# Down products one place later in the period, and one half of the hidden sums moved from GpSimd to VectorE

## What is computed

```python
s0 = relu(x @ swi[0]) @ swo[0]                    # 512 -> 2048 -> 512
s1 = relu(x @ swi[1]) @ swo[1]
eo = relu(x @ wi[type_label[b]]) @ wo[type_label[b]]
gate_in = concatenate([eo[:, 0], s0[:, 0], s1[:, 0]])        # first token of each batch entry
w = softmax(relu(gate_in @ g1) @ g2)                         # 3 weights for the entry
x = x + eo * w[0] + s0 * w[1] + s1 * w[2]
x = x + x @ W[cat_ids[b]] + b[cat_ids[b]]
```

## Time and profile before

| | us |
|---|---|
| median of 3 runs | 2041.92 |
| lowest, highest | 2038.39, 2043.65 |
| profiled execution | 2036.01 |
| its span, first to last instruction | 2034.2 |

### The profile page before, as it was taken

How to read it: one execution, slowest core, us unless ns; L and a number is a source line. 1 busy time by engine, 2 the same in 40 slices (tenths; PEclk the granted TensorE clock), 3 DMA queues, 4 the chain that set the end, 5 groups by cost and what they waited for, 6 DMA issues and landing times.

```text
span 2034.2 us, 24901 instructions
## 1 busy us (share of the span) xinstructions
PE 1956.8 (96%) x8504; PEld 1603.7 (79%) x8504; DVE 1269.4 (62%) x1186; ACT 968.5 (48%) x1441; POOL 877.3 (43%) x607
## 2 busy tenths in 40 slices
PE   6999999999899999999999999998989999999998
PEld 5777777777788888888788888887768888888886
DVE  6787788687654565445744554578874655455545
ACT  5655665555553343334443444356544643334342
POOL 5757775677422232233522322366563322223223
PEclk8999999999999999999999999999999999999999
DMA  6657666766676776566686676577568866666653
GB/s 222 228 226 262 257 228 244 298 233 239 229 255 207 223 238 204 180 197 194 209 269 195 194 242 197 198 257 259 227 220 275 256 215 210 208 191 201 196 161 124
DMA packets 187024, 450.98 MB, mean 222 GB/s; under 512 B 16916, under 2 KB 57876, under 8 KB 180500
## 3 DMA queue, kind: packets, MB, share of 16 engines
q1 hardware_dynamic: 186900, 449.39, 65.3%
HBM read 308.81 MB, written 140.51 MB: 221 GB/s over the span
## 4 chain that ended last, share of the span: by engine, by line
PE 79%; DVE 7%; issue 5%; POOL 4%; DMA 3%; ACT 2%; SPq 0%; POOLq 0%; ACTq 0%; DVEq 0%
PE rps L1248 38%; PE ups L1248 37%; PE aps L1248 3%; DMA PDR<-in_L_cond_wo_dram 2%; DVE HL L963 2%; DVE WD L953 1%; POOL HT L609 1%; DVE WU L946 1%; POOL XT L556 1%; DVE ACC L980 1%; DVE XL L937 1%; DVE gacc L1027 0%; POOL XT L659 0%; DMA PDR<-in_L_cond_swo_dram 0%; DMA XT<-in_x_dram 0%
## 5 line engine op out<-in xcount | busy, mean ns | idle before, releaser
L1248 PE MATMUL rps<-HH,WD 128*128 128x512 f32 x2688 | 890.4, 393 | 39.8 <-issue 38.8
L1248 PE MATMUL ups<-XH,WU 128*128 128x512 f32 x2688 | 894.7, 393 | 33.5 <-DVE hid L993 10.0
L609 POOL TENSOR_TENSOR HT<-hid 128x512 f32<-128x512 f32 x192 | 270.0, 1406 | 957.5 <-PE rps L1248 856.3
L1248 PEld LDWEIGHTS rps<-HH,WD 128*128 128x128 f32 x2688 | 509.2, 189 | 155.3 <-issue 47.5
L1248 PEld LDWEIGHTS ups<-XH,WU 128*128 128x128 f32 x2688 | 508.7, 189 | 151.1 <-DVE hid L993 14.2
L1248 PE MATMUL ups<-XL,WU 128*128 128x512 f32 x1344 | 527.0, 392 | 0.0
L1248 PE MATMUL rps<-HL,WD 128*128 128x512 f32 x1344 | 526.7, 392 | 0.0
L963 DVE TENSOR_TENSOR HL<-HT,HH 128x1024 fp32r<-128x1024 f32 x240 | 311.9, 1320 | 50.3 <-POOL HT L609 32.8
L983 DVE SCALAR_TENSOR_TENSOR ACC<-rps,gw,ACC 128x1024 f32<-128x1024 f32 x129 | 165.4, 1282 | 281.9 <-PE rps L1248 281.9
L1248 PEld LDWEIGHTS rps<-HL,WD 128*128 128x128 f32 x1344 | 254.6, 189 | 52.3
L1248 PEld LDWEIGHTS ups<-XL,WU 128*128 128x128 f32 x1344 | 254.6, 189 | 51.9
(11 more groups left out here) (102 smaller groups left out, 1487.2 us busy)
## 6 DMA issues: line engine op xcount, KB each, us to landing
WU<-wu_kept SPq DMA_DIRECT2D x448, 256.0 KB, 3.3
WD<-wd_kept SPq DMA_DIRECT2D x224, 512.0 KB, 3.4
wd_kept<-WD SPq DMA_DIRECT2D x112, 512.0 KB, 3.1
wu_kept<-WU SPq DMA_DIRECT2D x32, 1024.0 KB, 5.8
wu_kept<-WU SPq DMA_DIRECT2D x32, 768.0 KB, 3.3
sums_kept<-ACC SPq DMA_DIRECT2D x28, 512.0 KB, 5.0
MB<-sums_kept SPq DMA_DIRECT2D x28, 512.0 KB, 5.8
PUR<-in_L_cond_swi_dram SPq DMA_DIRECT2D x16, 512.0 KB, 7.0
```

Source lines behind the costliest of these rows:

```text
L609: pool.tensor_tensor(dst, p, q, op).then_inc(s_T, 1)
L1248: ins = pe.matmul(dst, stationary[a], moving[c], start=start and j == 0, stop=stop and j == 2, skip_group_check=True)
```

## The change

The diff does four things. (1) `place_of` moves every down product, with its addition, spill, kept and loaded down weights, one place later: place i of pass m now holds product i-1 of step m, place 0 product 6 of step m-1; the very last product follows the loop. The sums of gate, mixing and first token that hang on it move with it. (2) `hidden_sum` takes the engine as an argument. The four sums of half b run on VectorE at the start of the pass, in the order 0, 1, 3, 2; those of half a stay on GpSimd, the last of them (3) now at the start of the next pass. Each half has its own semaphore. (3) The orders change: high parts 3, 2, 6, 4, 5 and low parts 3, 1, 2, 6, 4, 5; `first_down_product` stands behind `chain(a)`, `relu_11(a)` and `scale_sums`; the addition of product 6 of the step before stands behind four sums and low parts 3, 1, 2 on VectorE. On GpSimd both `up_sums` go ahead of the hidden sums, and the token sums 0 and 1 follow them, 2 goes ahead of `down_sums`. (4) `made_after` makes down weights 0 and 1 of a prepared step together at place 5 (before: at places 3 and 4), the others one product later in step with the slots; `blocks_down` and `down_sums` have waits to fit.

```diff
-HI_ORDER = [0, 1, 6, 2, 3, 4, 5]
-LO_ORDER = [0, 6, 1, 2, 3, 4, 5]
+HI_ORDER = [0, 1, 3, 2, 6, 4, 5]
+LO_ORDER = [0, 3, 1, 2, 6, 4, 5]
...
+T_COUNT = [(1, 2, 3, 4), (1, 2, 4, 3)]
...
+def place_of(m, i):
+
+    return divmod(PRODUCTS * m + i - 1, PRODUCTS)
...
+def made_after(m, i):
+
+
+    e = down_of(m, i) + WD_SLOTS
+    made = {PRODUCTS - WD_SLOTS: [], PRODUCTS - WD_SLOTS + 1: [e - 1, e]}.get(i, [e])
+    return [k for k in made if k >= 0 and prepared(k // PRODUCTS)]
...
-        s_T = sem("hidden_sums")
+        s_T = [sem("hidden_sums_0"), sem("hidden_sums_1")]
...
-                    sp.wait_ge(s_wld, PRODUCTS * PREP[N])
+                    sp.wait_ge(s_wld, PRODUCTS * PREP[N] - 1)
+                    sp.wait_ge(s_Sd, 4 * PREP[N])
...
-                    e = down_of(m, i) + WD_SLOTS
+                    e = down_of(*place_of(m, i)) + WD_SLOTS
                     if e >= 0 and e // PRODUCTS < STEPS and not prepared(e // PRODUCTS):
                         load_down(e // PRODUCTS, e % PRODUCTS)
-                    if d >= 0 and spilled(d) and i >= 1:
+                    past, which = place_of(m, i - 1)
+                    if past >= 0 and spilled(past):
                         for j in range(SUMS):
-                            if SUM_LAST[j] == i - 1:
-                                spill(d, j)
-                    if e - 1 >= 0 and prepared((e - 1) // PRODUCTS):
-                        keep_down((e - 1) // PRODUCTS, (e - 1) % PRODUCTS)
+                            if SUM_LAST[j] == which:
+                                spill(past, j)
+                    for k in made_after(past, which):
+                        keep_down(k // PRODUCTS, k % PRODUCTS)
...
+        def hidden_sum(eng, N, half, which):
...
+                eng.wait_ge(s_T[half], 4 * N + T_COUNT[half][0])
...
+            eng.tensor_tensor(dst, p, q, op).then_inc(s_T[half], 1)
...
+                if PREP[N] > 0:
+                    pool.wait_ge(s_wld, PRODUCTS * PREP[N])
...
                 if d >= 0:
-                    for which in range(4):
-                        hidden_sum(d, 1, which)
+                    hidden_sum(pool, d, 0, 3)
                 if prepared_half(2 * N + 1):
                     up_sums(2 * N + 1)
-                if N < STEPS:
-                    hidden_sum(N, 0, 0)
-                    hidden_sum(N, 0, 1)
-                if end:
-                    token_sum(pool, super_of(m) + 1, 0)
                 if prepared_half(2 * N + 2):
                     up_sums(2 * N + 2)
                 if end:
+                    token_sum(pool, super_of(m) + 1, 0)
                     token_sum(pool, super_of(m) + 1, 1)
                 if N < STEPS:
-                    hidden_sum(N, 0, 2)
+                    hidden_sum(pool, N, 0, 0)
+                    hidden_sum(pool, N, 0, 1)
+                if end:
+                    token_sum(pool, super_of(m) + 1, 2)
                 if prepared(N):
                     down_sums(N)
-                if end:
-                    token_sum(pool, super_of(m) + 1, 2)
                 if N < STEPS:
-                    hidden_sum(N, 0, 3)
+                    hidden_sum(pool, N, 0, 2)
...
                 def second(i):
 
-                    if d >= 0:
-                        begin_sum(d, i)
-                    e = down_of(m, i) + WD_SLOTS
-                    if e >= 0 and prepared(e // PRODUCTS):
+                    step, which = place_of(m, i)
+                    if step >= 0:
+                        begin_sum(step, which)
+                    for e in made_after(step, which):
                         down_high(e // PRODUCTS, e % PRODUCTS)
 
-                if d >= 0:
-                    hidden_high(d, 6)
                 if more:
                     first_product(a)
                 if d >= 0:
-                    hidden_high(d, 2)
+                    hidden_high(d, 3)
                 if more:
                     seventh_product(a)
                 if m == -1:
...
                     for i in (4, 3, 5, 6):
                         token_high(0, i)
                 if d >= 0:
-                    first_down_product(d)
-                    hidden_high(d, 3)
+                    hidden_high(d, 2)
+                if start:
+                    token_high(s + 1, 5)
                 second(0)
+                if d >= 0:
+                    hidden_high(d, 6)
                 if more:
                     chain(a)
                 if start:
-                    token_high(s + 1, 5)
+                    token_high(s + 1, 6)
                 if more:
                     relu_11(a)
                 if d > 0 and super_of(d) % 2 == 1 and rel == 1:
                     scale_sums(d)
                 if d >= 0:
-                    hidden_high(d, 4)
+                    first_down_product(d)
                 if prepared_half(b):
                     up_high(b, 0)
                 second(1)
-                if start:
-                    token_high(s + 1, 6)
+                if d >= 0:
+                    hidden_high(d, 4)
                 if more:
                     relu_22(a)
                 if d >= 0:
...
                 for ms, c, stage in mixing[0]:
...
-                after = {1: 8, 2: 8, 3: 6}
+                after = {1: 3, 2: 3, 3: 1}
                 if i in after:
-                    dve.wait_ge(s_T, 8 * N + after[i])
+                    for half in range(2):
+                        dve.wait_ge(s_T[half], 4 * N + T_COUNT[half][after[i]])
...
-                    dve.wait_ge(s_T, 8 * (N - 1) + 4 * half + 1)
+                    dve.wait_ge(s_T[half], 4 * (N - 1) + T_COUNT[half][0])
+                    dve.wait_ge(s_hlo, PRODUCTS * (N - 1) + LO_ORDER.index(6) + 1)
...
+                if d >= 0:
+                    for which in (0, 1, 3, 2):
+                        hidden_sum(dve, d, 1, which)
                 if start:
                     token_low(s + 1, 2)
                     token_low(s + 1, 3)
                 if d >= 0:
-                    hidden_low(d, 6)
-                if d >= 0:
+                    hidden_low(d, 3)
                     hidden_low(d, 1)
                     hidden_low(d, 2)
                 if start:
                     token_low(s + 1, 5)
                 second(0)
+                if d > 0 and slice_of(d) == 0 and super_of(d - 1) % 2 == 0:
+                    first_token(super_of(d - 1) // 2, net_of(d - 1))
                 if d >= 0:
-                    hidden_low(d, 3)
+                    hidden_low(d, 6)
+                if start:
+                    token_low(s + 1, 6)
                 if prepared_half(b):
                     up_low(b, 0)
                 second(1)
                 block_22(a)
                 out_part(0, 0)
-                block_21(a)
-                mix(0, 0)
-                if start:
-                    token_low(s + 1, 6)
                 if d >= 0:
                     hidden_low(d, 4)
                 second(2)
+                block_21(a)
+                mix(0, 0)
+                if d >= 0:
+                    hidden_low(d, 5)
+                if prepared_half(b):
+                    up_low(b, 1)
                 mix(0, 1)
                 for ms, c, stage in mixing[0]:
                     if stage == 1:
                         mix_low(ms, c)
-                if d >= 0:
-                    hidden_low(d, 5)
-                if prepared_half(b):
-                    up_low(b, 1)
                 second(3)
-                if gating:
-                    gate_terms(s // 2)
                 out_part(0, 1)
...
-            for i in (6, 1, 2, 3):
+            for which in (0, 1, 3, 2):
+                hidden_sum(dve, t0, 1, which)
+            for i in (3, 1, 2):
                 hidden_low(t0, i)
+            add_sum(t0 - 1, 6)
+            hidden_low(t0, 6)
...
-                pe.wait_ge(s_hlo, PRODUCTS * N + (1, 3, 4, 5, 6, 7, 7)[i])
+                pe.wait_ge(s_hlo, PRODUCTS * N + LO_ORDER.index(i) + 1)
...
-                    if d >= 0:
-                        down(d, i)
-                    if gating and i == 2:
+                    step, which = place_of(m, i)
+                    if step >= 0:
+                        down(step, which)
...
+            down(STEPS - 1, PRODUCTS - 1)
```

83 lines of the change are left out of this document (38 added, 45 removed).

## The result

| | before | after |
|---|---|---|
| median of the runs, us | 2040.16 | 2018.35 |
| lowest, highest | 2037.66, 2043.65 | 2017.75, 2020.81 |
| span of the profiled execution | 2034.2 | 2016.0 |

The ratio is 0.9895, with an interval of 0.9879 to 0.9912: 1.05% faster. The forecast was 2011, in a range of 1992 to 2036. The medians are 21.8 us apart and the spans 18.2, since the profiled execution lay 4.2 under its median before and 0.6 under it after. All that follows counts in spans, where the forecast was -30.6: so 12.4 us of the expected gain are missing, and the question is where.

What follows compares the result with a forecast made beforehand. TensorE was taken to bound steady periods, VectorE's queue, a 40.4 us loop, the prepared ones. Terms for start, prepared, token and steady periods and end summed to -30.6 us: profiled execution 2036.0 to 2005, median 2011, range 1992 to 2036.

Steps and rivals of the forecast that it cites:

- Down products later: TensorE's down product 1 starts 13.6 us into the period instead of 8.2, so stalls like its 1.95 us go.
- The `PDR` wait: ScalarE's 5.95 us wait for the load of `PDR` goes, as weights 0 and 1 are made 10.9 us later.
- Section A: VectorE's stretch from the late low parts to the end of `block_22(a)`: 15.8 us becomes 16.8, bounds 16.0 and 17.8.
- Section B: TensorE from up(a,6) to the end of down product 4, six up and three down products: 16.3 us.
- Section C: From the end of down product 4 to the next late low parts: 6.4 us, bounds 5.7 to 6.9.
- The loop: VectorE's queue through TensorE and back in prepared periods: 39.5 us against 40.4 before, bounds 38.1 and 41.0.
- The strict form of the exclusion: Two-input VectorE and SBUF-reading GpSimd instructions exclude each other entirely: each of four sums 1.4 us, not 1.2; loop 40.4.
- The new wait of the copies: ScalarE's `first_down_product` waits for product 6's addition; down product 1 at 16.6 us, `block_22(a)` done at 16.8, almost level.
- The turns: Periods with token parts after prepared stretches: 91.0 to 86.3 us for 11 and 12, 44.4 to 42.7 for 36.
- the loop stays at 40.3: Rival, chance 0.24: section A at 17.7 us, two level limits and strict exclusion; total -20.9 us, 2021.
- TensorE bounds again: Rival, chance 0.14: loop 38.3 us, GpSimd's four sums leaving the contended stretch free more; total -46.4, 1996.
- The slower rival: Rival, chance 0.10: section A's instructions stay slowed, product 6's addition becomes the path; A 20.3, loop 43, total 2053.

Runs made afterwards that it cites:

- sums_only: The kernel before, with half b's four hidden sums on VectorE at the start of its list, places as before: 2052.7 us, ratio 1.0057.
- weights_apart: The kernel after, with down weights 0 and 1 made one by one at places 4 and 5, not both at 5: 2012.22 us, ratio 0.9862.
- add6_early: The kernel after, with the addition of product 6 of the step before ahead of hidden low part 2 on VectorE: 2019.28 us, ratio 0.9884.
- places_only: The kernel after, with all eight hidden sums of a step on GpSimd, places and orders as changed: 2034.52 us, ratio 0.9974.
- turn_vector: The kernel after, with token low parts 2 and 3 ahead of the four sums on VectorE where new tokens begin: 2015.17 us, ratio 0.9875.
- turn_both: The kernel after, with token low parts 2 and 3 ahead of VectorE's four sums and GpSimd's last token sum ahead of down sums: 2015.66 us, ratio 0.9867.
- best1: The kernel after with `block_21(b)` earlier, weights_apart, turn_both, `scale_sums` behind `first_down_product`, and the last step's product 6 addition ahead of low parts: 1999.96 us, ratio 0.9791.

## Why the prediction was right, and where its sum was off

Point by point, by the steps of the prediction.

- *(1) Down products later.* Right. Down product 1's large stalls are gone, and the new limits stand where they were expected: the copies, and `u`, which the working had 0.4 us late and which is 0.47 late in most plain periods, though a wait for `u` was also listed as a sign of being wrong. sums_only shows the other side of it: without the later place, +12.
- *The `PDR` wait.* Gone, as said. But the means, two weights made together at place 5, were more than it took: with one place weights_apart has the wait in 4 periods instead of 15, in two of them at no cost, and is 6 us faster.
- *(2) Section A.* 16.8 forecast, 15.8 measured. The mis-sized term is the four sums: 4.8 us with each slowed to 1.2, measured 3.7 (1.22, 1.04, 0.69, 0.68 with their small waits). GpSimd's weight sums needed 3.7 us (289.09 to 292.83) instead of 6.8, so two of the sums had nothing beside them. The prediction had applied the slowed price to both sides at once.
- *(3) Section B.* 16.3 forecast, 16.5 measured.
- *(4) Section C.* 6.4 forecast, 7.6 measured, outside its bounds of 5.7 to 6.9. The term is the two down low parts: 1.0 each, measured 3.18 for both, beside GpSimd's down sums. The row that was nearest, 1.18 for one of them, was below what two in a row cost.
- *The loop.* 39.5 forecast (38.1 to 41.0), 39.9 measured: two errors of 1.0 and 1.2 that nearly cancel. The strict form of the exclusion in the Trainium skill, page "SBUF — State Buffer", section "Who interferes with whom", gave 40.4. (By the prediction's own terms it is 40.3: 0.2 more for each of four sums.) The rows lie between: sums of 1.22 and 1.04 where they meet GpSimd, 0.68 where they don't. But taken together the two engines come out near exclusion: from 290.00 to 293.37, 3.37 us, VectorE did three instructions of 0.68 alone and GpSimd two of 0.73 alone, 3.5 us of work by that estimate, and both were slowed.
- *The new wait of the copies.* Expected "two limits almost level", and they are. The copies are the later one, by 0.2 us (up(a,6) starts at 303.45, `block_22(a)` ends at 303.26), and add6_early turns them round.
- *Periods 8 to 10.* -6.4, exact. *33 to 35:* -9.0 forecast, -10.5 measured. *24:* -2.0 and -3.3. Here the clock is at 1.00 in all three stretches, against 0.96 to 0.99 before: it came back whole and not by half.
- *The turns.* The largest error: 11 and 12 together took 88.9 instead of 86.3, and 36 took 48.75 instead of 42.7. Time also moved between neighbours: against the kernel before, 11 is 7.2 shorter and 12 is 5.0 longer (44.51 to 49.55), 35 is 4.0 shorter and 36 is 4.3 longer. The step that failed is "token low parts come 2.8 us later behind the four sums", in two terms. The sums took 6.7 us in both turns, up to 2.65 for one, since GpSimd was making token sums and hidden sums beside them; in sums_only, without that, they took 2.8. And GpSimd's last token sum, to which the prediction gave no term, ended 5.9 us later in the period than before: with no sums ahead of the token low parts TensorE still waits 5.96 us (places_only) and 5.97 (turn_vector), and VectorE 3.52 for that sum. On top, the idle piece of 8.1 us brought the lower clock, some 2 us more, which the prediction had counted as going away. With both out of the way (turn_both) the wait is 2.46, but the four sums are late for ScalarE and `u`, and the period is 48.29. VectorE's list alone isn't the bound, since places_only has four sums fewer on it and turns of 50.1. What bounds the turn beyond these waits, and how much of it is the slowing and how much the length of the lists, stays open.
- *Start and end.* The wait in front of up(0b,6) went, but 2.58 and 2.48 us stand in front of up(1a,1) and up(1a,2), so the start gave 1.7 less than forecast. At the end the stall for the copies was forecast at 4.3 and measured 4.53. The other 1.1 of the 1.3 missing there are mostly the clock: from this stall to the end it is 0.94 over 45.3 us, before 0.96 over 44.2, which makes about 1 us, an estimate from these two means.
- *`scale_sums`.* Counted at +2.0 in the sum against -1.8 for steady periods. It cost 1.7 in each of periods 14 and 38 (best1), and the steady stretches gave back about 0.6 each, of the 0.9 counted.

The sum, in differences to the forecast: turns +8.6, plain periods +2.8, start and end +3.0, steady stretches +2.0, and -4.0 for periods 24, 32 and 33 to 35: +12.4. Of the rivals, "the loop stays at 40.3" gave 2021, and in spans -20.9: it is 2.7 us from the total, the forecast 12.4. Its loop is no nearer than that of the forecast, 39.9 being midway between 39.5 and 40.3, and its reason is wrong: A is 15.8, not 17.7, and what kept the loop above 39.5 is C. Most of the shortfall is at the turns, the start and the end, which the rival priced as the forecast did. So the total came near the rival by luck, and the forecast holds with the loop right within 0.4 us and the turns wrong. Some terms can't be worked out again: -9.0 for 33 to 35 and -2.0 for 24 are given without their working, and the rival "TensorE bounds again" has 10.8 and 13.2 where a loop of 38.3 by the other lines' arithmetic makes 10.0 and 12.6. The slower rival didn't come: no prepared period from 2 on is longer than 41.4 us outside the turns.

What the two parts of the change do for each other is not additive. In plain periods the later place, with its orders, gives the gain, and the engine of the sums doesn't matter (39.6 against 39.9). The sums on VectorE pay where GpSimd's own queue is late: the first steps, new tokens, gate periods, the end.

## What to carry to other kernels

A move of work from one engine to another pays where the giving engine's queue is late, not where its busy share is high: look for the stretches in which someone waits for it. Price each moved instruction once for every kind of stretch, by what runs beside it there; here the same four sums took 3.7 us in one and 6.7 in another, and the second figure was a part of the largest error. The other part was an item of the giving engine's own list, which came later in the period: look at both queues. And when two limits are level, one experiment that takes one away shows nothing but the other: shorten the loop that both hang on (`block_21(b)` first gave 10 us).

## What the runs showed of the hardware that was not expected

- A VectorE sum of 128x512 with both inputs in SBUF takes 0.68 us alone, 1.04 to 1.22 beside GpSimd's weight sums of 128x256, and up to 2.65 beside its sums of 128x1024 and 128x512. So the slowing is not a fixed amount.
- It goes with the work that GpSimd does beside it: with 192 sums taken off GpSimd, VectorE's other instructions are 109.4 us shorter than in places_only, where all else is the same. Additions with one input in PSUM were left at 1.22 us in the kernels before and after, in places_only and in sums_only.
- After 8.08 us idle TensorE ran at a granted clock of 0.50 (1.2 GHz) over the next 4 us; up(12a,2) took 2.9 us instead of 1.5.
